# Three reordered VectorE steps in an eight-round graph network: fixed one-hots, statistics and a multiply pass change places

## What is computed

```python
x = _layernorm(x + _L0_gnn_ref(x, edge_index, ...))                 # three mean-aggregating (SAGE) layers
x = _layernorm(x + _L1_gnn_ref(x, edge_index, edge_attr_16, ...))   # one layer with edge features (GIN)
x = _layernorm(x + _L2_gnn_ref(x, edge_index, edge_weight, ...))    # two degree-normalised layers (GCN), each with its own norm
x = _layernorm(x + _L3_gnn_ref(x, ..., src, dst, edge_type_8))      # two relational layers, eight edge types (RGCN)
```

## Time and profile before

| what | value |
|---|---|
| median of 3 runs | 5315.82 us (5305.98 to 5324.11) |
| the profiled execution's own time | 5309.55 us |
| its span in the profile | 5307.4 us |
| mean granted clock of TensorE | 0.945 |
| busy: PE, PEld | 4370.0, 2877.0 us |
| busy: DVE, ACT, POOL | 3367.0, 2416.1, 1938.6 us |
| chain that ended last | PE 47%, issue 15%, DVE 12%, ACT 8%, DVEq 6%, POOL 5%, DMA 3% |

### The profile page before, as it was taken

One profiled execution on the slowest core, in us unless ns is written; L12 is line 12 of the kernel. 1 busy time (PEld: TensorE's weight loads), 2 busy tenths in 40 slices (PEclk: granted clock), 3 DMA queues, 4 the chain that ended last, 5 costly groups with the idle time before them and its releaser, 6 DMA issues.

```text
span 5307.4 us, 129128 instructions
## 1 busy us (share of the span) xinstructions
PE 4370.0 (82%) x25128; PEld 2877.0 (54%) x25129; DVE 3367.0 (63%) x10608; ACT 2416.1 (46%) x4969; POOL 1938.6 (37%) x1886
## 2 busy tenths in 40 slices
PE   6998898777788888867777688886899996888986
PEld 4664554444355555545554355543677773676763
DVE  6554443787545555458886688875466664777775
ACT  2442442555267777536664466654122211333333
POOL 5650782663033333026540534400433312333310
PEclk9999999898799999989999899998999998999998
DMA  4663784665244444335552566653444433434332
GB/s 141 217 211 124 250 263 169 199 203 191 86 130 146 147 152 143 109 112 175 172 168 93 167 215 210 213 175 105 143 137 137 137 104 115 125 123 127 111 110 89
DMA packets 443917, 815.60 MB, mean 154 GB/s; under 512 B 70872, under 2 KB 76818, under 8 KB 443828
## 3 DMA queue, kind: packets, MB, share of 16 engines
q1 hardware_dynamic: 389172, 697.28, 39.1%
q0 software_dynamic: 54656, 117.32, 8.9%
HBM read 480.10 MB, written 334.22 MB: 153 GB/s over the span
## 4 chain that ended last, share of the span: by engine, by line
PE 47%; issue 15%; DVE 12%; ACT 8%; DVEq 6%; POOL 5%; DMA 3%; ACTq 3%; SPq 1%; POOLq 0%
PE p_agg L1133 8%; PE p_edge L1120 7%; PE p_agg L1135 7%; PE p_tr L1120 6%; POOL raw L697 4%; PE p_agg L1166 4%; DVE stats L1679 3%; DVE onehot L1576 2%; ACT u L917 2%; ACT o L898 2%; PE p_wide L1253 2%; PE p_dense L1209 2%; PE p_agg L1159 2%; PE p_dense L1185 2%; PE p_dense L1187 2%
## 5 line engine op out<-in xcount | busy, mean ns | idle before, releaser
L1133 PE MATMUL p_agg<-onehot,msg 128*128 128x512 f16 (+1 forms) x2848 | 1128.9, 396 | 547.1 <-issue 233.8
L697 POOL DMA_INDIRECT raw<-node_s,src_i x980 | 971.8, 992 | 1387.2 <-DMA node_s<-o 554.1
L1135 PE MATMUL p_agg<-onehot,msg 128*128 128x512 f16 (+1 forms) x2848 | 1128.3, 396 | 0.0
L1576 DVE TENSOR_SCALAR onehot<-iota,place 128x512 f16<-128x512 f16 x2058 | 698.8, 395 | 371.2 <-PE p_agg L1166 315.3
L1133 PEld LDWEIGHTS p_agg<-onehot,msg 128*128 x2848 | 281.0, 99 | 887.2 <-issue 737.6
L697 POOL DMA_INDIRECT raw<-node_x,src_i x392 | 381.3, 973 | 541.5 <-DMA feature<-more_masked 253.4
L898 ACT ACTIVATE o<-v_ring,nmr,rstd 128x128 f32 (+1 forms) x1176 | 472.8, 482 | 86.9 <-DVE nmr L1695 81.8
L1567 DVE TENSOR_SCALAR onehot<-iota,dst_f,negbase 128x512 f16 (+1 forms) x790 | 317.4, 448 | 280.1 <-PE p_agg L1135 181.1
L1679 DVE BATCH_NORM_STATS2 stats<-v_ring 128x6 f32 (+1 forms) x1960 | 418.6, 279 | 106.0 <-DVE v_ring L1668 55.6
L1166 PE MATMUL p_agg<-h_in,w 128*128 128x512 f32 x784 | 436.4, 640 | 41.6 <-DMA h_in<-feature 39.9
L917 ACT ACTIVATE u<-v_ring,nmr,rstd 128x128 f32 (+1 forms) x784 | 312.5, 481 | 218.6 <-DVE res_in L1725 147.5
(11 more groups left out here) (262 smaller groups left out, 8025.4 us busy)
## 6 DMA issues: line engine op xcount, KB each, us to landing
node_s<-o SPq DMA_DIRECT2D x392, 256.0 KB
h_in<-feature SPq DMA_DIRECT2D x392, 256.0 KB
feature<-u SPq DMA_DIRECT2D x294, 256.0 KB
node_x<-o SPq DMA_DIRECT2D x294, 256.0 KB
res_in<-node_x SPq DMA_DIRECT2D x294, 256.0 KB
h_in<-node_s SPq DMA_DIRECT2D x196, 256.0 KB
h_t<-dinv_scratch SPq DMA_DIRECT2D x196, 256.0 KB, 3.4
h_in<-in_x SPq DMA_DIRECT2D x98, 256.0 KB
```

What stands on the lines that cost most here:

```text
L697: nc.gpsimd.indirect_dma_start(out=raw[:, (e % RING) * BATCH + j, :], out_offset=None, in_=src_d, in_offset=bass.IndirectOffsetOnAxis(ap=s ...
L1133: nc.tensor.matmul(p_agg[:, a, :], tile_ap(msg, t, 0, D), oh, start=first, stop=True, skip_group_check=True)
L1135: return nc.tensor.matmul(p_agg[:, a, :], tile_ap(msg, t, D, 2 * D), oh, start=False, stop=True, skip_group_check=True)
L1576: last = V.tensor_scalar(tile_ap(onehot, EVERY * a + j), iota[:, :], place[:, bass.ds((it * 2 + a) * EVERY + j, 1)], None, ALU.is_equal)
```

## The change

The edit moves calls within three hand-written orders of VectorE and changes nothing else. In the third round the second half's degree sum and fixed one-hots go between the residual add and its statistics; in the fifth the second half's fixed one-hots go ahead of the multiply pass by the gain; in the eighth the first half's fixed one-hots (of the pair after the next) go between the add and its statistics.

```diff
@@ first_gcn_step @@
                     statistics(it, 0)
                     statistics(it, 1)
+                    fixed(it + 2, 1)
                     gain_pass(it - 1)
-                    fixed(it + 2, 1)
                     scale_and_move(it)
@@ mean_step @@
                     statistics(it - 1, 0)
                     add(it - 1, 1)
                     these = list_of(it + 1)
-                    statistics(it - 1, 1)
                     degrees(it, 1)
                     fixed(it + 1, 1)
+                    statistics(it - 1, 1)
                     scale_and_move(it - 1)
                     add(it, 0)
@@ second_relational_step @@
                     add(it, 1)
                     these = list_of(it + 1)
+                    fixed(it + 2, 0)
                     statistics(it, 1)
-                    fixed(it + 2, 0)
                     take_in(these)
```

## The result

The changed kernel takes 5342.56 us (median; 5341.08 to 5344.2) against 5315.82: 0.5% longer, ratio 1.005 with a 95% interval of 1.0038 to 1.0063. The forecast was 5337.0, slower. The profiled execution took 5341.08 us (span 5338.9), 31.5 more than the profiled one of before.

The account below looks back on a forecast made before the run. VectorE's order was taken as the bound; third round 19.2, fifth 0 and eighth 2.2 us sum to 21.4 us slower, 5331 from the profiled execution, 5337 as a median. Range 5314 to 5360 us.

Parts of the forecast that it names:

- The bound: Third round's steady part: VectorE's order, with the gaps in which it has nothing issued, sets the step.
- The square root: Third round: ScalarE's square root loses its cover, so the reciprocal shows about 0.37 us idle in every step.
- The degree sum's own issue: Third round: the moved degree sum's wait and address cost 0.24 us where the list's gap shows; about 0.10 gained where hidden.
- The cycle: Third round's steady part: two batches in three steps lose 0.35 + 0.69 = 1.04 us; nine cycles lose 9.4.
- the collision: Rival, third round: shifted one-hots run into GpSimd's multiply, 2 us in each of ten cycles, 5357 us; chance 0.12.
- whose gap is hidden: Third-round step where VectorE's sequencer has run ahead, hiding the list read: loses 0.35 us, against 0.69 where the gap shows.
- The other steps: Third round, some 14 steps before and after the steady stretch: 0.6 us each, 8.4 us lost.
- The dense end: Third round's end: statistics wait behind the degree sum, which waits for the last matmuls; reciprocal 1.4 us later.
- The fifth round at zero: Multiply pass and one-hots change places, the reciprocal starts when it did: zero, bounds 4.4 us gain or as much loss.
- the eighth at 2.2 us: Eighth round: earlier one-hots are waited for at the feature load; extra one-hots 0.45 us later in five last steps.
- No net effect: Rival: subtraction's stretching takes up the loss, degree sum issued under the add; 5316 to 5325 us; chance 0.25.
- TensorE as the bound: Rival, third round: 31 one-hot waits shrink by 1.4 us each and VectorE follows; 43 us faster, 5273; chance 0.08.

Follow-up runs that it names:

- degree sum alone: Kernel before, with only the third round's degree sum moved ahead of the statistics, one-hots left behind them: ratio 0.9999, third round 494.7 us.
- list at the root: Third round's edit alone, with the next step's list read between statistics and reciprocal: ratio 0.9995 to the kernel before, third round 492.5 us.
- the add as the cover: Third round's edit alone, with the next step's first residual add moved ahead of the reciprocal: ratio 1.0016 to the kernel before, third round 504.8 us.
- eighth hunk alone: Kernel before with only the eighth round's edit: ratio 1.0002, eighth round 845.2 us against 836.4.
- third hunk: Kernel before with only the third round's edit: ratio 1.0058 (1.0044 to 1.0071), third round 517.1 us against 494.2.
- the first cover: Kernel before, with the sixth round's second-half fixed one-hots moved between statistics and reciprocal: ratio 0.9976, sixth round 764.9 us against 786.0.
- the last kernel of the sixth round: Sixth-round one-hots moved ahead of the reciprocal; second reciprocal put off into the next step, behind the list read, ahead of the multiply by the gain: 0.9879, 5249.34 us.

## Why the prediction was right, and where it was not

**The bound** was right: VectorE's order sets the third round's step. TensorE got its one-hots in another order and waits for them as long as before (60.5 us in the earlier trace rows, 63.5 after).

**The square root** was right to the hundredth: 0.37 us idle, then 18.0 / 49 = 0.37 in every step. Two kernels that restore the cover or put other necessary work into that wait (degree sum alone, list at the root) show a third round as short as before; with the add as the cover it is 10.6 us longer. In the sixth round the cover by itself took 21.1 us off.

**The degree sum's own issue** was taken at +0.24 where the gap shows and -0.10 where it is hidden. In the nine cycles the statistics start 0.16 us after the end of a list's read that shows, and in the changed kernel the degree sum 0.36 us after it: 0.20, so the size was right. With the degree sum alone ahead, the gaps grow by 62.1 - 52.8 = 9.3 us in the round; in the changed kernel they do not grow (52.9): in seven of the nine cycles a held one-hot hides the read behind it. Neither the one-hots that gave it back in the first nor the hiding in the second was counted.

**The cycle** is the term that was off in size: 1.04 us forecast, 15.0 / 9 = 1.67 measured. Of the 15.0 us, the reciprocal's idle time makes 9.9; one-hots are busy 11.7 longer and subtractions 4.8 less; the idle time ahead of statistics and degree sums falls by 1.2. The uncovered square root and the shorter hold of the subtraction are the forecast's; the held one-hots are not. I had "with 0.35 us added they end 0.29 before it", so the collision stood as a rival with 0.12. In seven of the nine cycles it happened. From the end of the long subtraction to GpSimd's multiply is 8.79 us before (1206.90 + 3.00 to 1218.69) and 8.78 after (1221.65 + 2.47 to 1232.90), but the one-hots start 7.95 us after it instead of 7.16 (1232.07, against 1217.06): a shift of 0.79 us, over the 0.64 that the text itself named as the limit. The step behind a long subtraction was not one "whose gap is hidden": there the degree sum (1226.89) showed 0.54 us of idle where the statistics had shown 0.14. The collision's price was not 2 us a cycle either, since behind the held one-hot the gaps ahead of the statistics and the degree sum are hidden: the two cycles without a collision take 28.62 us each, the seven with one 29.19 on average, 0.57 more. Even without it a cycle loses 1.22 us, and there the long subtraction gives back 0.5 us (2.49 instead of 2.99), where the forecast had it take up a whole 0.69.

**The other steps**, cut at each step's first aggregation, were forecast at 8.4 us and made 9.0: 3.7 ahead of the nine cycles (944.95 to 1021.3, then 945.98 to 1026.0), 5.3 in the nine steps behind them (1267.9 to 1358.5, then 1287.6 to 1383.5): 17 steps at 0.53 us, where the forecast had 14 at 0.6. The dense end was forecast at +1.4 and made -1.1. Third round: 19.2 forecast, 22.8 measured. That the sum comes so near is in part luck: the cycles were taken 5.6 us too low and the dense end 2.5 too high.

**The fifth round at zero** and **the eighth at 2.2 us** are not contradicted, and not shown either: alone they measure 0.9999 and 1.0002, and 2.2 us is less than these intervals can tell. The forecast's mechanism for the eighth can be seen in its waits. Of TensorE's in the changed kernel:

```profile
PE p_agg L1166 <- DMA h_in<-feature: 45.4, 16, 4.1
PE p_agg L1133 <- DVE onehot L1567: 29.3, 10, 5.2
PE p_agg L1133 <- DVE onehot L1576: 22.7, 14, 1.9
```

Before they were 39.4, 23.9 and 32.8 us: 10.1 us less for fixed one-hots, 6.0 more for the feature load and 5.4 more for extra one-hots. With the eighth hunk alone they are 46.3, 29.6 and 22.3. That is the forecast's "what is gained is waited for there", and its later extra one-hots.

**The rivals.** No net effect fell with the third hunk's interval, TensorE as the bound with the earlier trace rows and their counterpart. The collision did come, on top of the forecast's mechanism and at a price of 0.57 us in seven cycles instead of 2 in ten.

**The signs.** Of the three signs of being wrong, one came: one-hots of over 2 us in the steady part. The second, VectorE waiting for matmuls there, stands in the profile eight times but is the list's read each time; the third, a third round of no more than 510 us, did not come. Of the signs of being right, the 0.37 us at the reciprocal came in every step, and the gap moved from the statistics to the degree sum (not wholly: 11.5 us stay). In the nine cycles a step without a batch took 8.26 us on average; it now takes 8.66 without a collision, within the 0.35 to 0.7 forecast, and 9.23 with one.

## What to carry to other kernels

A pair of reductions, a square root on another engine and a reciprocal has a wait in it (0.37 us in the third round, 0.47 at the second norm of the sixth): on an engine that sets the pace, put work that is ready anyway between them, and when moving such work away, price the wait that it covered from a place where nothing covers it. An instruction moved to cover one wait may open another that it covered before, as the add did, so look for a second wait of the same engine (a list read, control work) to lie beside the first, as the list and the root here. And a shift of half a microsecond can bring an instruction with two SBUF operands, or a one-hot pass, under GpSimd's multiply: look where both stand in every stretch of the cycle before and after.

## What the runs showed of the hardware that I had not expected

- The sequencer's read of three words takes between 534 and 1620 ns in the changed kernel's third round (50 reads, median 1104): the same instruction, threefold spread.
- A scalar-tensor-tensor instruction on 128x8 values takes 0.17 us, and 0.62 when it begins 1.11 us into GpSimd's multiply (sixth round with the first cover, 3192.99 and 3191.88): held until that multiply's end, small as it is.
- A one-hot pass that starts 0.57 us before the profile shows GpSimd's multiply (1232.33 and 1232.90), and normally takes 0.35, is held until that multiply's end all the same: 2.42 us. Just ahead of the multiply, GpSimd was issuing its last gather (1231.93 to 1232.88); the one-hot pass before, at 1232.07 beside that gather, was not held (0.35 us). So when the hold begins is not shown by the start of the multiply's record.
- The time from a subtraction's end to the multiply that GpSimd starts in its wake hardly varies (8.77 to 8.92 us in the nine cycles of both kernels), so the hold falls on whatever VectorE has in that place: subtractions before, one-hots with the list at the root, both in the changed kernel. In the last kernel of the sixth round that place has instructions that are hardly held, and the multiply by the gain takes 20.4 us less (80.2 to 59.8).
